# Both expert layers' first products: exact float32 matmuls replaced by three float32r passes over split operands

## The chip, the cores and the metric

The kernel runs on one core of a Trainium2 chip. The metric is the device time of one execution in microseconds (us). TensorE (PE) multiplies, VectorE (DVE) and ScalarE (ACT) work on tiles in SBUF and PSUM, GpSimd (POOL) issues the indirect transfers and SyncE (SP) most of the others. Every engine runs its own instruction list in order and waits on semaphores.

## The reference

Sixteen images of 256x256 pass through a wavelet stage, one attention layer, a first expert layer, a cosine "circuit" layer with a small feed-forward net, and a second expert layer, with a layer normalisation after each. Only the two expert layers matter here. Their core is, cut down:

```
# first expert layer: 4096 tokens, 8 experts, the best 2 of each token, hidden width 512
h = relu(einsum('nc,ech->neh', xf, w1) + b1)
expert_out = einsum('neh,ehc->nec', h, w2) + b2
out = einsum('ne,nec->nc', weights, expert_out)
# second expert layer: 8 experts, the best 1 of each token, hidden width 1024
h = gelu(einsum('ecd,edf->ecf', eb, W1) + b1[:, None, :], approximate=False)
y = einsum('ecf,efd->ecd', h, W2) + b2[:, None, :]
```

All inputs and outputs are float32; a token has 256 numbers.

## The kernel before

The stages follow each other: `attention`, `experts` (the first expert layer), `middle`, `last_experts` (the second). Between stages every engine waits for the others (`quiet0`, `quiet1`, `quiet2`).

Both expert stages work on tiles of 128 rows that all belong to one expert: 71 tiles in `experts`, 39 in `last_experts`. Rows were scattered to DRAM grouped by expert; a tile's rows come back by an indirect gather on POOL. The number of the tile's expert is computed on the chip (`tile_maps`, DVE) and read into a register of each engine that needs it (`value_load`). The computation of these maps is in two builds: the first 8 tiles (`maps_ok`), then the rest (`all_maps`).

One tile goes through these steps, and the order on PE is written out by hand:

- `g1(j)`: the first product, the transposed rows `xT` (128x128 twice) as stationary operand and the expert's first weights, 512 columns at a time, as moving operand. In `experts` that is two float32 matmuls (L1291), in `last_experts` four (L2054), in two halves of 512 columns.
- `x2(j+1)`: two PE transposes of the next tile's rows (L1282, L2042), which ACT copies into `xT` (L1338, L2100).
- `g2(j-1)`: the second product of the tile before, in four (L1303) or eight (L2065) float32 matmuls of 256 columns.
- `th(j)`: transposes of this tile's hidden values (L1313, L2075), which ACT passes through Relu (L1344) or Gelu (L2108, one instruction of 512 columns for each half).

DVE adds the first bias when it copies the first product out of PSUM (`eh`, L1383 and L2138), finds in `owner` which rows are whose (L1371 to L1376, the last one scales the row by a gate), and adds the second bias and combines in `g2` (L1392, L1396; L2147 to L2161). In `last_experts` it also normalises (`end`, L2169), after POOL has computed the root.

SBUF is cut into zones that the stages reuse. The first experts' weights take 64 KB a partition, the last experts' all 128 KB. Weights of four of the last experts are loaded during `middle`, the others at the start of `last_experts`.

Of the kernel before, what the change touches and what calls it, by code (L numbers as in the profile page):

```python
# [97 lines left out]
def tower(nc, a, out):  # L98
# [14 lines left out]
    def zones(stage):  # L113
        wide = Space(nc, low, W_BYTES, stage)
        return {"w": wide, "low": Space(nc, low, W_BYTES // 2, stage), "high": Space(nc, high, W_BYTES // 2, stage),
                "bias": Space(nc, bias, BIAS_BYTES, stage), "rest": Space(nc, rest, fixed - rest, stage),
                "open": Space(nc, bias, fixed - bias, stage), "free": Space(nc, bias + BIAS_BYTES // 4, fixed - bias - BIAS_BYTES // 4, stage)}

    with ctx:
# [21 lines left out]
        weights0 = zone0["low"]("w0", [P, E, 2 * F0 + F0 // P * D])  # L141
        zone_m = zones("_m")
        sb = zone_m["high"]
# [7 lines left out]
        bias1 = zone1["bias"]("b1", [P, E, F1 + D])  # L151
# [16 lines left out]
        def load_bias(sp, layer, to, e, landed):  # L168
            width = (F0, F1)[layer]
            for at, n, w in ((0, "b1", width), (width, "b2", D)):  # L170
                sp.dma_start(to[:, e, at:at + w], a[f"L{layer}_ffn_{n}"][e:e + 1, :].broadcast_to([P, w])).then_inc(landed, 16)

        def load_fixed(sp):
            for to, n in ((w2n, "attn_w2"), (w1n, "attn_w1"), (wg1, "ffn_wg")):
                sp.dma_start(to[:], a["L1_" + n].rearrange("(c p) k -> p c k", p=P)).then_inc(s["w_in_m"], 16)
            sp.dma_start(b1n[:], a["L1_attn_b1"].rearrange("(c p) -> p c", p=P), allow_slow_non_contiguous=True).then_inc(s["w_in_m"], 16)
# [3 lines left out]
        with nc.Block() as block:  # L180
            used = attention(nc, block, a, s, zones("_a"), ctx0, load_weights, lambda sp, e: load_bias(sp, 0, bias0, e, s["b_in0"]), h0_d, rows0_d, ident, before, ones, iota8, cnt,
                             lane, tile_no, ones8, sends0, minus_half)
            experts(nc, block, s, ctx, used, zone0, weights0, bias0, load_fixed, rows0_d, y0_d, cnt, ident, iota8, lane, tile_no, ones8)
            ctx0.close()
            middle(nc, block, a, s, ctx, zone_m, fixed_weights, load_weights, lambda sp, e: load_bias(sp, 1, bias1, e, s["w_in1"][e]), y0_d, rows1_d, ident, before, ones, iota8, cnt, away1, rank1, minus_half)
            last_experts(nc, block, s, ctx, zone1, weights1, bias1, load_weights, load_bias, rows1_d, gate1_d, out, cnt, rank1, away1,
# [3 lines left out]
def tile_maps(nc, c, sb, count, cnt, iota8, lane, tile_no, ones8):  # L190
# [40 lines left out]
    def maps(first_done, all_done):  # L231
        common()
        build(0, EARLY)
        c.eng.sem_inc(first_done, 1)
        build(EARLY, count)
# [4 lines left out]
def attention(nc, block, a, s, zone, sems, load_weights, load_bias, h0_d, rows0_d, ident, before, ones, iota8, cnt, lane, tile_no, ones8, sends0,  # L240
# [17 lines left out]
    with ExitStack() as psum:  # L258
# [8 lines left out]
        h1 = [sb(f"h1_{u}", [P, TPI, ROW0]) for u in range(2)]  # L267
        row_i = [sb(f"row_i{u}", [P, TPI, 2], I32) for u in range(2)]
# [5 lines left out]
        res = sb("res", [P, TPI, D])  # L274
        sb = zone["open"]
# [914 lines left out]
def experts(nc, block, s, ctx, used, zone, w, b, load_fixed, rows_d, y_d, cnt, ident, iota8, lane, tile_no, ones8):  # L1190
# [9 lines left out]
    xT = [sb(f"exT{u}", [P, 2, P]) for u in range(2)]  # L1200
    h = [sb(f"eh{u}", [P, width]) for u in range(2)]
# [4 lines left out]
    result = sb("result", [P, D])  # L1206
    sent_to = [sb(f"sent_to{u}", [P, 1], I32) for u in range(YR)]
# [5 lines left out]
        sem("e" + n) for n in ("xT_ps", "xT_ok", "g_ps", "h_ok", "t_ps", "hT_ok", "y_ps", "y_ok", "own_ok", "biased"))  # L1213
    y_out = [sem(f"ey_out{u}") for u in range(YR)]
    x_in, w_in = s["x_in0"], s["w_in0"]

    with ExitStack() as psum:
# [14 lines left out]
        def _(pool):  # L1232
            c = Chain(pool, s["pool_c"])
            pool.wait_ge(s["quiet0"], 4)
            for u in range(XR):
                c.run(nc.gpsimd.memset(x[u][:], 0.0))
            pool.wait_ge(c.sem, c.n)
            for u in (s["rows_out0"], s["rows_out0_odd"]):
# [3 lines left out]
            def load(j):  # L1242
                if j == EARLY:
                    pool.wait_ge(all_maps, 1)
                if j >= XR:
                    pool.wait_ge(xT_ps, j - XR + 1)
                    pool.wait_ge(own_ok, j - XR + 1)
# [17 lines left out]
        def _(pe):  # L1265
# [11 lines left out]
            def x2(j):  # L1277
                pe.wait_ge(x_in[j % XR], 16 * (j // XR + 1))
                if j >= 2:
                    pe.wait_ge(xT_ok, j - 1)  # L1280
                for ch in range(2):
# [3 lines left out]
            def g1(j):  # L1285
                e = number[j]
                pe.wait_ge(xT_ok, j + 1)
                if j >= 2:
                    pe.wait_ge(h_ok, j - 1)
                for ch in range(2):  # L1290
                    last = nc.tensor.matmul(bank[1 + j % 2][:], xT[j % 2][:, ch, :],  # L1291
                                            w[:, bass.ds(e, 1), width * ch:width * (ch + 1)].rearrange("p a f -> p (a f)"),
                                            start=ch == 0, stop=ch == 1)
# [902 lines left out]
```

## Time and profile before

| | |
|---|---|
| Median of 3 runs | 1461.22 us (1459.81 to 1462.4) |
| Profiled execution | 1454.15 us |
| Its span | 1452.4 us |
| PE busy | 1262.1 us (87%) |
| DVE busy | 950.5 us (65%) |
| POOL busy | 717.7 us (49%) |
| ACT busy | 522.8 us (36%) |

The span is what the trace covers. `experts` issues its first matmul at 512.9 us and its last near 809 us, `last_experts` runs from about 1116 us to the end. A float32 matmul appears in the trace as two records, each with its own weight load. A record's duration includes the way through the array, so that durations of neighbours overlap; the distance between starts says what one costs.

### The profile page before, as it was taken

The page shows a single profiled execution, that of the slowest core. Times are in us where ns is not written, and L with a number is a line of the kernel's source. Part 1 is how long each engine was busy: PE and PEld are TensorE (multiplying, and loading weights), DVE is VectorE, ACT ScalarE, POOL GpSimd, SP SyncE. Part 2 cuts the span into 40 slices and gives each one's busy share as a digit, 9 for nine tenths or more (in the row PEclk, how much of TensorE's full clock was granted, in tenths as well). Part 3 has the DMA queues.
Part 4 walks back from the last instruction along what each step waited for, and adds up shares of the span by engine and source line. Part 5 has one row for each costly group of instructions (what it writes and reads, how often), then busy time and mean ns, then how long its engine had stood idle before and what let it go on. Part 6 is the DMA issues. An engine that isn't in the chain of part 4 may idle for free. (4 is left out here: it accounts for less than half of the span.)

```text
span 1452.4 us, 23662 instructions
## 1 busy us (share of the span) xinstructions
PE 1262.1 (87%) x6856; PEld 895.0 (62%) x6856; DVE 950.5 (65%) x2759; ACT 522.8 (36%) x999; POOL 717.7 (49%) x912
## 2 busy tenths in 40 slices
PE   1389889889999589999999479999894999999997
PEld 0256556566665356666676357777773676767665
DVE  6678888887876455555555579999975344444443
ACT  1136455445555112222222366665651211111111
POOL 6673384472322344454454345666664354454543
PEclk9879899889998689999999777778876999999999
DMA  6566666567874414112121433321000910110000
GB/s 177 90 105 106 111 105 102 85 105 130 162 126 135 150 54 114 61 63 66 62 65 42 132 103 122 92 70 44 15 16 34 336 61 29 33 33 28 27 17 13
DMA packets 88619, 124.23 MB, mean 86 GB/s; under 512 B 17824, under 2 KB 71726, under 8 KB 87728
## 3 DMA queue, kind: packets, MB, share of 16 engines
q1 hardware_dynamic: 68704, 83.04, 26.9%
q0 software_dynamic: 16416, 38.46, 8.2%
q10 hardware_dynamic: 3376, 1.22, 0.4%
q8 instruction: 62, 1.02, 0.3%
q14 instruction: 61, 0.50, 0.1%
HBM read 69.14 MB, written 29.44 MB: 68 GB/s over the span
## 5 line engine op out<-in xcount | busy, mean ns | idle before, releaser
L1093 DVE TENSOR_REDUCE top_a_a<-s_bank 128x4 f32<-128x1024 f32 x128 | 156.4, 1222 | 51.2 <-PE s_bank L738 50.0
L2054 PE MATMUL ebank<-w,exT 128*128 x312 | 143.4, 603 | 0.7 <-ACT exT L2100 0.7
L1611 PE MATMUL mbank<-w2T_m,fhT_m 128*128 128x256 f32 x512 | 142.3, 441 | 0.0
L2065 PE MATMUL ebank<-w,ehT 128*128 x624 | 141.2, 379 | 0.9 <-ACT ehT L2108 0.9
L917 ACT ACTIVATE prob_a<-s_bank 128x1024 f32<-128x1024 f32 x128 | 130.7, 1021 | 19.5 <-PE s_bank L759 18.9
L1291 PE MATMUL ebank<-w,exT 128*128 x284 | 135.5, 600 | 0.6 <-ACT exT L1338 0.6
L1303 PE MATMUL ebank<-w,ehT 128*128 x568 | 134.4, 380 | 0.8 <-ACT ehT L1344 0.8
L1248 POOL DMA_INDIRECT ex<-rows_d,tile_row x71 | 72.4, 1020 | 123.6 <-DVE ey L1376 110.6
L1611 PEld LDWEIGHTS mbank<-w2T_m,fhT_m 128*128 128x128 f32 x512 | 118.3, 231 | 22.9
L2065 PEld LDWEIGHTS ebank<-w,ehT 128*128 128x128 f32 x624 | 115.6, 190 | 15.7 <-issue 1.6
L649 POOL DMA_INDIRECT rows_d<-h_a,row_i_a x64 | 64.2, 1003 | 98.6 <-DVE row_i_a L1178 86.7
L1383 DVE TENSOR_TENSOR eh<-ebank,b 128x512 f32<-128x512 f32 x71 | 49.1, 691 | 96.2 <-PE ebank L1291 96.2
L1303 PEld LDWEIGHTS ebank<-w,ehT 128*128 128x128 f32 x568 | 102.5, 190 | 12.5 <-issue 1.5
L2138 DVE TENSOR_TENSOR eh<-ebank,b 128x512 f32<-128x512 f32 x78 | 53.9, 691 | 77.4 <-PE ebank L2054 77.4
L2054 PEld LDWEIGHTS ebank<-w,exT 128*128 128x128 f32 x312 | 57.3, 194 | 58.7 <-issue 58.7
L2108 ACT ACTIVATE ehT<-ebank 128x512 f32<-128x512 f32 x78 | 42.3, 594 | 138.6 <-PE ebank L2075 138.6
L1253 POOL DMA_INDIRECT y_d<-ey,sent_to x71 | 72.8, 1025 | 34.8 <-issue 20.4
L738 PE MATMUL s_bank<-ks_a,qs_a 48*128 48x256 f32 x512 | 67.4, 343 | 25.9 <-DVE top_a_a L1093 14.7
L1344 ACT ACTIVATE ehT<-ebank 128x512 f32<-128x512 f32 x71 | 42.4, 597 | 131.0 <-PE ebank L1313 131.0
L2147 DVE TENSOR_TENSOR ey<-ebank,b 128x256 f32<-128x256 f32 x39 | 16.6, 425 | 95.1 <-PE ebank L2065 95.1
L1522 POOL TENSOR_SCALAR rstd_m_m<-moments_m_m 128x2 f32<-128x2 f32 x64 | 25.9, 404 | 105.8 <-DVE minus_m_m L1789 75.8
L771 PE MATMUL av_bank<-prob_a,vx_a 128*32 128x256 f32 x1024 | 77.8, 427 | 0.4 <-ACT heads_a L924 0.4
(348 smaller groups left out, 2662.8 us busy)
## 6 DMA issues: line engine op xcount, KB each, us to landing
w<-in_L_ffn_W SPq DMA_DIRECT2D x16, 1024.0 KB, 10.4
qs_a<-parts_q_a SPq DMA_DIRECT2D x96, 128.0 KB, 4.5
ks_a<-parts_k_a SPq DMA_DIRECT2D x96, 128.0 KB
w<-in_L_ffn_w SPq DMA_DIRECT2D x16, 512.0 KB, 5.6
image_a<-in_x SPq DMA_DIRECT2D x4, 1024.0 KB, 7.8
ya_m<-y_d SPq DMA_DIRECT2D x16, 256.0 KB, 2.8
yb_m<-y_d SPq DMA_DIRECT2D x16, 256.0 KB, 3.1
b<-in_L_ffn_b SPq DMA_DIRECT2D x8, 512.0 KB, 8.9
```

Of the source, the lines that this page charges most:

```text
L649: pool.indirect_dma_start(out=rows0_d, out_offset=bass.IndirectOffsetOnAxis(ap=row_i[i % 2][:, t, k:k + 1], axis=0), in_=h1[i % 2][:, t, : ...
L738: last = nc.tensor.matmul(s1_bank[:, g, t * SEQ:(t + 1) * SEQ], qs[i % RING][rows, j, t * P:(t + 1) * P], ks[i % RING][rows, j, :], start= ...
L771: last = nc.tensor.matmul(av_bank[32 * j:32 * j + 32, 0:SEQ], vx[i % RING][:, t, head(k, j), :], prob[:, (2 * k + j % 2) % 4, j // 2, t, : ...
L917: nc.scalar.activation(prob[:, j % 4].rearrange("p g t s -> p (g t s)"), s2_bank[:].rearrange("p g s -> p (g s)"), ACT.Exp, scale=HD ** -0 ...
L1093: nc.vector.tensor_reduce(top[:, j].rearrange("p g t -> p (g t)"), s1_bank[:].rearrange("p g (t s) -> p (g t) s", t=TPI), axis=AX, op=ALU. ...
L1248: pool.indirect_dma_start(out=x[j % XR][:].bitcast(I32), out_offset=None, in_=rows_d, bounds_check=E * SLOTS - 1, oob_is_err=False, in_off ...
L1253: pool.indirect_dma_start(out=y_d, out_offset=bass.IndirectOffsetOnAxis(ap=sent_to[j % YR][:], axis=0), in_=y[j % YR][:], in_offset=None, ...
L1291: last = nc.tensor.matmul(bank[1 + j % 2][:], xT[j % 2][:, ch, :], w[:, bass.ds(e, 1), width * ch:width * (ch + 1)].rearrange("p a f -> p ...
L1303: last = nc.tensor.matmul(bank[4 + j % 2][:, 0:D], hT[j % 2][:, f, :], w[:, bass.ds(e, 1), at:at + D].rearrange("p a d -> p (a d)"), start ...
L1611: last = nc.tensor.matmul(b[:, t * D:(t + 1) * D], hT[:, f, t * P:(t + 1) * P], w2T[:, f, :], start=False, stop=f == FC - 1)
L2054: last = nc.tensor.matmul(bank[1 + n % 2][:], xT[j % 2][:, ch, :], w[:, bass.ds(e, 1), at:at + 512].rearrange("p a f -> p (a f)"), start=c ...
L2065: last = nc.tensor.matmul(bank[4 + j % 2][:, 0:D], hT[j % 2][:, f, :], w[:, bass.ds(e, 1), at:at + D].rearrange("p a d -> p (a d)"), start ...
```

## The change

A float32r matmul takes one pass over its columns, at a lower precision of the operands. The change writes each operand of the first product as a near part (the value rounded to float32r) plus a rest (value minus near part), and adds three products: near by near, near by rest, rest by near. The code:

- In `experts`, ACT rounds all first weights into `w0_near` in 16 pieces of 512 columns, two a tile after `th(j)`, and DVE writes the rests into `w0_low`, two a tile behind `g2(j-1)`. Tiles 0 to 8 (`WHOLE` = 9) still use the float32 matmuls. From tile 9 on `g1` is six float32r matmuls in place of two float32 ones; ACT's copy goes to a float32r tile and DVE makes its rest (`xl`). The gate's scaling moves from DVE (L1376) to ACT (`scaled`), and a gather's buffer is now freed by it.
- In `last_experts` the two parts are made for each tile anew, one tile ahead: ACT reads the next tile's expert number, copies the expert's column of first biases (`own_bias`), and rounds 4 pieces of 512 columns (`rounded`); DVE makes the 4 rests (`rest`), interleaved with the copies out of PSUM. `g1` is twelve float32r matmuls in place of four float32 ones and waits for the rests. The first bias moves from DVE's copy to the Gelu, which becomes 8 instructions of 128 columns with a bias operand instead of 2 of 512.
- At the start of `last_experts` the first tile's rests come between the two builds of the maps.
- The first biases of the last experts are loaded as columns (8 small transfers in `load_fixed`), no longer broadcast to all partitions. SBUF zones are laid out anew; `middle` computes the same.

```diff
@@ experts, PE
             def g1(j):
                 e = number[j]
-                pe.wait_ge(xT_ok, j + 1)
+                if j < WHOLE:
+                    pe.wait_ge(xT_ok, j + 1)
+                if j >= WHOLE:
+                    pe.wait_ge(xl_ok, j + 1 - WHOLE)
+                if j == WHOLE:
+                    pe.wait_ge(low_ok, len(PIECES))
...
+                    if j < WHOLE:
+                        last = nc.tensor.matmul(to, xT[j % 2][:, ch, :], own[0], start=ch == 0, stop=ch == 1)
+                    else:
+                        nc.tensor.matmul(to, xTn[j % 2][:, ch, :], own[0], start=ch == 0, stop=False)
+                        nc.tensor.matmul(to, xTn[j % 2][:, ch, :], own[1], start=False, stop=False)
+                        last = nc.tensor.matmul(to, xTl[j % 2][:, ch, :], own[0], start=False, stop=ch == 1)
...
@@ experts, ACT
+            def scaled(j):
+                u = j % YR
+                act.wait_ge(own_ok, j + 1)
+                nc.scalar.activation(y[u][:], x[j % XR][:, 0:D], ACT.Identity, bias=nought[:, 0:1], scale=own[u][:, 2:3]).then_inc(scaled_ok, 1)
+            def near(n):
+                e, at = PIECES[n]
+                if at == 0:
+                    act.wait_ge(w_in[e], 32)
+                nc.scalar.activation(wn[:, e, at:at + PIECE], w[:, e, at:at + PIECE], ACT.Copy).then_inc(near_ok, 1)
...
@@ experts, DVE
             for j in range(count + 1):
                 if j < count:
                     g1(j)
+                if WHOLE <= j + 1 < count:
+                    xl(j + 1)
+                if j < count:
                     owner(j)
                 if j >= 1:
                     g2(j - 1)
+                    for n in range(2 * j - 2, min(2 * j, len(PIECES))):
+                        low(n)
...
@@ last_experts, PE
             def g1(j):
                 e = number[j]
                 pe.wait_ge(q["w_ready"], e + 1)
-                pe.wait_ge(q["xT_ok"], j + 1)
+                pe.wait_ge(q["xl_ok"], j + 1)
+                pe.wait_ge(q["low_ok"], PER * (j + 1))
...
@@ last_experts, ACT
             def th(j):
...
-                    nc.scalar.activation(hT[j % 2][:, at:at + 4].rearrange("p c s -> p (c s)"), bank[6 + n % 2][:], ACT.Gelu)\
-                        .then_inc(q["hT_ok"], 1)
+                    for f in range(4):
+                        last = nc.scalar.activation(hT[j % 2][:, at + f], bank[6 + n % 2][:, f * P:(f + 1) * P], ACT.Gelu, bias=b1[j % 2][:, at + f:at + f + 1])
+                    last.then_inc(q["hT_ok"], 1)
...
             for j in range(count):
                 if j + 1 < count:
+                    own_bias(j + 1)
+                    for k in range(PER - 1):
+                        rounded(j + 1, k)
                     x2(j + 1)
+                    rounded(j + 1, PER - 1)
+                act.wait_ge(q["b1_ok"], j + 1)
                 th(j)
...
@@ last_experts, DVE
-            maps(q["maps_ok"], q["all_maps"])
+            maps(q["maps_ok"], q["all_maps"], first_rest)
...
+            xl(0)
             for j in range(count + 2):
                 if j < count:
-                    g1(j)
+                    for n in range(FB):
+                        if j + 1 < count:
+                            rest(j + 1, n)
+                        g1(FB * j + n)
+                if j + 1 < count:
+                    xl(j + 1)
+                    for k in range(FB, PER):
+                        rest(j + 1, k)
                 if j >= 2:
                     end(j - 2)
```

## Rows read from the trace of the kernel before

**Rows 1.** The page, chain that ended last: shares of the span by line.

```profile
PE ebank L2054 9%; PE ebank L2065 9%; PE ebank L2075 2%; PE ebank L2042 1%; DMA ex<-rows_d,tile_row 0%; DVE row_f L225 0%; PE mbank L1629 0%; POOL out_tower L2008 0%; PE mbank L1621 0%; DVE r_m L1869 0%; DVE z_m L1860 0%; DVE stats_m_m L1779 0%; POOL rstd_m_m L1526 0%; POOL rstd_m_m L1524 0%; DVE eh L2138 0%
```

**Rows 2.** Busy time by window: PE, PEld, DVE, ACT, POOL, then PE clock, DMA.

```profile
530.00:600.00 70.00, 70.00 (x309) 48.54 (x308) 39.60 (x120) 16.75 (x35) 34.99 (x35) 1.00 0.33 90
563.00:564.00 1.00, 1.00 (x6) 0.86 (x5) 0.87 (x5) 0.00 (x0) 0.03 (x1) 1.00 1.26 175
1250.00:1350.00 100.00, 100.00 (x432) 70.37 (x431) 42.88 (x99) 18.03 (x37) 49.46 (x63) 1.00 0.11 32
```

**Rows 3.** The chain in order of time, one tile of `last_experts`: start, us, what.

```profile
1143.02 3.43 PE ebank L2054 x8
1146.45 0.22 PE ebank L2042 x2
1146.67 3.46 PE ebank L2065 x16
1150.13 0.87 PE ebank L2075 x8
```

**Rows 4.** Timeline of one tile of `experts`: start, us, engine, line, what.

```profile
605.38 0.42 DVE L1392 TENSOR_TENSOR result<-ebank,b 128x256 f32<-128x256 f32 x1 [0.41 <-PE ebank L1303]
605.51 1.88 PE L1291 MATMUL ebank<-w,exT 128*128 x4
605.84 0.48 DVE L1396 SCALAR_TENSOR_TENSOR ey<-result,own,ey 128x256 f32<-128x256 f32 x1
607.23 0.38 PE L1282 MATMUL ebank<-ident,ex 128*128 128x128 f32 x2
607.61 0.69 DVE L1383 TENSOR_TENSOR eh<-ebank,b 128x512 f32<-128x512 f32 x1 [1.28 <-PE ebank L1291]
608.21 0.22 DVE L1371 SCALAR_TENSOR_TENSOR chosen<-ex,tile_sum 128x6 f32<-128x6 f32 x1
```

**Rows 5.** Timeline of `middle`: four float32r matmuls of 256 columns, 80 rows.

```profile
987.18 0.72 PE L1595 MATMUL mbank<-qT_m,wq_m 80*128 80x256 f32 x4
```

**Rows 6.** Groups by line and shape: count, busy us, mean ns, idle before.

```profile
L2100 ACT ACTIVATE exT<-ebank 128x256 f32<-128x256 f32 x39 | 15.0, 384 | 124.7 <-PE ebank L2042 124.7
L895 ACT ACTIVATE parts_k_a<-bank,bk_a 128x256 fp32r<-128x256 f32 x32 | 13.4, 471 | 31.6 <-PE bank L715 31.6
L1702 ACT ACTIVATE arg_size_m<-arg_m 128x512 f32<-128x512 f32 x16 | 10.1, 631 | 5.1 <-DVE arg_m L1809 5.1
L1818 DVE TENSOR_TENSOR sum_m<-prods_m,h_m 128x512 f32<-128x512 f32 x16 | 11.1, 692 | 0.5
```

**Rows 7.** Timeline: transposes and Gelu of one late tile; two ScalarE instructions behind each other.

```profile
1325.60 1.04 PE L2075 MATMUL ebank<-ident,eh 128*128 128x128 f32 x8
1326.30 1.09 ACT L2108 ACTIVATE ehT<-ebank 128x512 f32<-128x512 f32 x2 [3.57 <-PE ebank L2075]
332.67 0.84 ACT L895 ACTIVATE parts_k_a<-bank,bk_a 128x256 fp32r<-128x256 f32 x2 [1.29 <-PE bank L715]
```

**Rows 8.** PE's reading of a tile's expert number (L1275): ns min/median/max.

```profile
L1275 PEldq TENSOR_LOAD <-tile_expert x71: 297/369/510, 506.0 to 797.5; - x71
L1275 PEldq FUSED_REGOPS  x71: 151/151/165, 506.6 to 797.9; - x71
```

**Rows 9.** Timeline, start of `last_experts`: second map build, last DVE step, first product.

```profile
1121.87 0.42 DVE L218 TENSOR_TENSOR past<-tile_no,upto 128x248 f32<-128x248 f32 x1
1125.60 0.42 DVE L2124 TENSOR_REDUCE den<-exps 128x32 f32<-128x256 f32 x1
1126.55 0.18 DVE L2128 TENSOR_SCALAR outside<-outside 128x39 f32<-128x39 f32 x1
1126.84 6.65 PE L2054 MATMUL ebank<-w,exT 128*128 x8 [0.67 <-ACT exT L2100]
```

**Rows 10.** Two DVE lines, all instances: ns min/median/max.

```profile
L1396 DVE SCALAR_TENSOR_TENSOR ey<-result,own,ey x71: 483/485/494, 523.8 to 809.9; 128x256 f32<-128x256 f32 x71
L225 DVE TENSOR_SCALAR row_f<-row_f,lane x4: 231/246/2022, 504.8 to 1124.2; 128x8 f32<-128x8 f32 x2, 128x63 f32<-128x63 f32 x1, 128x31 f32<-128x31 f32 x1
```

More of the change, by code:

```diff
@@ L116, in zones @@
                 "bias": Space(nc, bias, BIAS_BYTES, stage), "rest": Space(nc, rest, fixed - rest, stage),
-                "open": Space(nc, bias, fixed - bias, stage), "free": Space(nc, bias + BIAS_BYTES // 4, fixed - bias - BIAS_BYTES // 4, stage)}
+                "open": Space(nc, bias, fixed - bias, stage),
+                "after": Space(nc, bias + 4 * E * (F0 + D) + 32 * (F1 // P), fixed - bias - 4 * E * (F0 + D) - 32 * (F1 // P), stage),
+                "above": Space(nc, bias + 4 * E * (F0 + D), BIAS_BYTES - 4 * E * (F0 + D), stage)}
     with ctx:
@@ L234, in maps @@
         c.eng.sem_inc(first_done, 1)
+        if between:
+            between()
         build(EARLY, count)
@@ L1350, in _ @@
                 th(j)
+                scaled(j)
+                for n in range(2 * j, min(2 * j + 2, len(PIECES))):
+                    near(n)
             nc.scalar.drain().then_inc(s["quiet1"], 1)
@@ L1919, in last_experts @@
     out_v = out.rearrange("i s d -> (i s) d")
-    sb = zone["rest"]
+    PIECE, PER = 512, 2 * width // 512
+    near = [zone["bias"](f"near{u}", [P, 2 * width], F32R) for u in range(2)]
+    sb = zone["after"]
+    low = [sb(f"low{u}", [P, 2 * width], F32R) for u in range(2)]
+    b1 = [sb(f"b1_own{u}", [P, FC]) for u in range(2)]
     x = [sb(f"ex{u}", [P, WIDE_ROW]) for u in range(XR)]
-    xT = [sb(f"exT{u}", [P, 2, P]) for u in range(2)]
+    xT, xTl = ([sb(f"{n}{u}", [P, 2, P], F32R) for u in range(2)] for n in ("exT", "exTl"))
     h = [sb(f"eh{u}", [P, 512]) for u in range(HR)]
@@ L2053, in g1 @@
                         at = width * ch + 512 * (n % FB)
-                        last = nc.tensor.matmul(bank[1 + n % 2][:], xT[j % 2][:, ch, :],
-                                                w[:, bass.ds(e, 1), at:at + 512].rearrange("p a f -> p (a f)"), start=ch == 0, stop=ch == 1)
+                        to, whole, rest = bank[1 + n % 2][:], near[j % 2][:, at:at + 512], low[j % 2][:, at:at + 512]
+                        nc.tensor.matmul(to, xT[j % 2][:, ch, :], whole, start=ch == 0, stop=False)
+                        nc.tensor.matmul(to, xT[j % 2][:, ch, :], rest, start=False, stop=False)
+                        last = nc.tensor.matmul(to, xTl[j % 2][:, ch, :], whole, start=False, stop=ch == 1)
                     last.then_inc(q["g_ps"], 1)
@@ new lines, in first_rest @@
+            def first_rest():
+                dve.wait_ge(q["exps_ok"], 1)
+                c.link(nc.vector.tensor_reduce(den[:], ex[:], axis=AX, op=ALU.add))
+                c.link(nc.vector.reciprocal(den[:], den[:]))
+                nc.vector.scalar_tensor_tensor(out=gates[:], in0=rank[:], scalar=float(CAP), in1=den[:], op0=ALU.is_lt, op1=ALU.mult)\
+                    .then_inc(q["gates_ok"], 1)
+                for k in range(PER):
+                    rest(0, k)
+            maps(q["maps_ok"], q["all_maps"], first_rest)
```

142 lines of the change are left out of this document (92 added, 50 removed).

## The prediction

> **What bounds the kernel now.** I read the chain of waits first: it is PE almost alone, and PE's four lines of `last_experts` hold 21% of the span, the stage's whole length [rows 1]. The busy time by window then says where PE has no gap: 70.00 of 70 us in `experts` and 100.00 of 100 in `last_experts`, both at a granted clock of 1.00, its 2.4 GHz level [rows 2]. In these stretches time is the sum of what PE has in its list, and no other engine is waited for. ACT is busy 24% and 18% there, DVE 57% and 43%. The chain in order of time gives a late tile: first product 3.43, `x2` 0.22, second product 3.46, `th` 0.87, together 7.98 us for each of 39 tiles [rows 3]. In `experts` the first product takes 607.23 - 605.51 = 1.72 us [rows 4]; with `x2` 0.22, half the late tile's second product (1.73) and half its `th` (0.44), all from [rows 3], a tile takes 4.1 us, 71 times. So what shortens the first product shortens the kernel, as long as nothing else becomes late.
>
> **Price of a float32r pass.** A float32 matmul of 512 columns is two records, 3.43/8 = 0.43 us apart, so 0.86 us each [rows 3]. Float32r matmuls are in the trace with 256 columns and 80 rows: four take 0.72 us, and less about 0.28 for the last one's way through the array that is 0.44/3 = 0.15 between starts on average, a first handover among them [rows 5]. The second product's records also go through 512 columns (two times 256) in 3.46/16 = 0.216 us. I take 0.215 us for a pass of 512. Twice the 0.15 would be 0.29, and the far end is 0.43, the spacing of one float32 record, if operands of 128 rows cannot be streamed faster. I take the row with as many columns, since columns are what the float32 records' spacing follows (256 twice 0.216, 512 twice 0.43).
>
> **`experts`.** From tile 9 on `g1` is six passes, 6 x 0.215 = 1.29, in place of 1.72 us: 0.43 less for each of 62 tiles, **-26.7 us**. The other engines have room. DVE gets `xl` (0.43, as the 256 columns of L1392) and loses L1376; ACT gets `scaled` and, until tile 7, two pieces of 0.63 us a tile (as L1702 [rows 6]), against a tile of 4.1 us of which it uses a quarter. `x2` is ready 1.3 us into a tile, ACT's copy takes 0.38 [rows 6], DVE's `eh` and `xl` end by about 2.8 of 3.67, so `g1(j+1)` finds its rest.
>
> One wait is not hidden. Tile 9's `g1` wants all 16 rests, and the last two are behind `g2(7)` on DVE in the turn of tile 8. In the turn shown, the same step (L1396) starts 0.33 us after PE's `g1` and ends at 606.32 [rows 4]; in the tile numbering of the change that `g1` is tile 9's. Two rests of 0.69 us (L1818 [rows 6]), 0.61 apart as L1383 and its successor are [rows 4], end at 606.32 + 0.61 + 0.69 = 607.62, against a start at 605.51: **+2.2 us**, once. It is 0 if the queue turns out shorter.
>
> **`last_experts`, PE.** Twelve passes are 2.58 in place of 3.43 us: a tile of 7.12 us if nothing waits, 0.86 less.
>
> **`last_experts`, the loop through ACT and DVE.** Here two lightly used engines get most of PE's relief as work. ACT: 8 Gelus of 128 columns with a bias. 256 columns without one take 0.384, with one 0.471, and the second of two starts 0.84 - 0.47 = 0.37 behind the first [rows 6, 7]; L2108's pair gives 0.49 for 512 columns [rows 7]. That is 0.83 ns a column, so a Gelu of 128 costs 0.37 - 0.11 = 0.26 to 0.27 between starts and 0.37 in full. Rounding takes 0.63 in full (L1702 [rows 6]) and about 0.53 between starts. Reading the expert number is 0.37 + 0.15 and small change on PE [rows 8]; I take 0.6. ACT's sum is 8 x 0.27 + 4 x 0.53 + 0.3 + 0.6 + 0.15 = 5.3 us of 7.1. DVE has 42.88/100 x 7.98 = 3.4 us a tile now [rows 2] and gets 4 x 0.69 + 0.43 = 3.2: 6.6 busy, less where neighbours overlap. Neither sum exceeds PE's, but both lists are in order, and this path closes over two tiles:
>
> - `th(j-1)` starts at 0. ACT's first Gelu starts 0.70 later (1326.30 against 1325.60 [rows 7]), the eighth 7 x 0.27 later, at 2.6.
> - Behind it the expert number, 0.6, and the bias copy: 3.4. The first near part of tile j+1 is ready at about 4.1.
> - DVE waits for it in front of both `eh` copies of tile j. With 0.2 for the wait and the address (L1383 starts 0.22 after PE's end at 607.39 [rows 4]), rest 0, `eh`, rest 1, `eh`, `xl`, rest 2, rest 3 start at 4.3 + 0, 0.61, 1.22, 1.83, 2.44, 2.78, 3.39, and the last ends at 8.38.
> - `g1(j+1)` can start at 8.44, and `th(j+1)`, the same step two tiles on, 7.12 - 0.87 = 6.25 later.
>
> Two tiles then take 8.44 + 6.25 = 14.69, one 7.35 us, more than PE's 7.12. So I expect DVE's rests to be waited for about 0.2 us a tile and a gain of 7.98 - 7.35 = 0.63 over 38 periods: **-23.9 us**. Bounds: no wait at all, -32.7. With no overlap of Gelus (0.37 each) the path is 0.7 longer; with 0.2 more per rest (L1396's 0.485 for 256 columns, doubled, is the nearest row with overheads counted twice) 0.8 more. Both give (14.69 + 1.5)/2 = 8.1 and +4.6.
>
> One rule of the Trainium skill speaks against DVE's new work: GPSIMD Engine Reference, section Specifications, says that POOL's SBUF interfaces are shared with VectorE and contend with its instructions that have two SBUF inputs, which every rest is. The trace shows such a hold-up: L225, 0.23 us elsewhere, took 2.02 while POOL filled buffers, though it has one tensor input; it also shows L1396, with two SBUF inputs and next to POOL's gathers, at 483 to 494 ns in all 71 instances [rows 10]. By the rows the rests keep 0.69 us; by the rule each could be held by a gather's issue.
>
> **Start of `last_experts`.** Before, DVE makes the second map build under the first gather's flight, 1121.87 to 1125.60, and ends at 1126.73; `g1(0)` starts at 1126.84 [rows 9]. Now the first rests come between the builds. ACT reads the number and rounds four pieces from 1121.8: 0.6 + 0.15 + 3 x 0.53 + 0.63, so 1124.8; the last rest starts at 1125.1, the second build at 1125.7, and takes 3.7; `outside` and `xl(0)` 0.6, so `g1(0)` starts at about 1130.1: **+3.3 us**. The tail after the last tile's products is unchanged.
>
> **At nothing.** Eight bias columns are 8 x 1024 elements of 4 bytes on SP's queue, which has no other work then; PE was busy 1.00 of 1 us at a DMA share of 1.26 while the like was loaded [rows 2]. If gathers are held longer than the buffers last, a few us. The gather's buffer is freed about 2 us later by `scaled`; four buffers of 3.67 us cover this. The gate's scaling on ACT, bias adds, new zones and the larger count in `middle`'s waits are off PE's path. A dynamic address now stands before six matmuls; PE reads ahead of its array, cover that would cost tenths of a us a tile if gone.
>
> **Sum.** -26.7 + 2.2 - 23.9 + 3.3 = -45.1 us. The profiled execution would be 1454.15 - 45.1 = 1409. It is 7.1 us below the median of the runs; the same difference on that median gives 1461.22 - 45.1 = **1416 us**.
>
> **The rivals.**
> - *No wait on the rests.* If reading the number overlaps the last Gelus, the path is up to 0.5 shorter and PE alone bounds: -26.7 + 2.2 - 32.7 + 3.3 = -54, 1407. For it: both sums are below 7.1. Against: the rests stand before and behind both copies in order. 0.15.
> - *ACT and DVE bound the last experts*, 7.6 to 8.1 us a tile: between -36 and -17, 1426 to 1445. For it: three new handovers whose latency I priced from two rows. 0.2.
> - *Slower, by POOL.* POOL issues three indirect transfers a tile at 1.0 us. If the rests wait for them, DVE's 6.6 us become 9.6 and set the tile: -24.5 + 38 x 1.6 + 3.3 = +40, 1501. The gain is gone from 8.5 us a tile on. L1396 speaks against, L225 for it [rows 10]. It is what the rule named above, of the Trainium skill's GPSIMD Engine Reference, would do here. 0.05.
> - *Slower, by the pass.* If a float32r pass of 128 rows costs 0.43, the first products grow by 62 x 0.86 + 39 x 1.73 = 121 us, 1582. The change would then not do what it says. Against: the spacing with 80 rows [rows 5]. 0.04.
> - *No change, by the pass.* At 0.29 us a pass the first products take 3.48 and 1.74 us, as now; with the two delays that is 1461 + 8 at most, within 0.5%, and about the same if one of them is smaller. 0.02.
> - My forecast, 7.2 to 7.6 us a tile, 1410 to 1426: 0.54.
>
> **The range.** 1403 to 1438: down to no wait with a free start, up to most of the second rival; 0.13 lies outside, the two slower rivals among it. A run of this kernel tells about 0.2%, 3 us, from no change. Faster by more: 0.89; within it 0.02 (a pass of nearly 0.29 us); slower 0.09.
>
> **What would show each step.** Passes in `g1` 0.215 us apart in both stages; `g1` to `g1` 4.1 us until tile 8 and 3.67 after; one gap near 2 us before tile 9; in `last_experts` PE idle about 0.2 us a tile before `g1`, released by DVE's rest, alternating or even; the ACT list full to about 75%, rests at 0.69 us with and without POOL beside them; the first product of `last_experts` some 3 us later after the maps. I am wrong if rests are longer beside POOL, if PE waits for ACT's Gelu instead, or if the passes are further apart.

## The result and the profile after

The changed kernel takes 1424.68 us (median of 4 runs, 1422.47 to 1425.59), the kernel before in the same session 1460.51 (4 runs, 1459.12 to 1462.4): a ratio of 0.9752, 95% interval 0.9735 to 0.9769, so 35.8 us less. The forecast was 45.1 us less.

The profiled execution of the change is 1425.59 us long, only 28.6 less than the one of before. That difference can't be used as it stands. I cut both traces at the same matmuls (between the first two stages lie 12 us more, alike in all four). "The maps" is the first DVE step of `tile_maps` in `last_experts`:

| stage, us | before | change | second profile of each |
|---|---|---|---|
| start to last matmul of attention | 500.8 | 507.4 | 505.1, 502.7 |
| `experts`, first to last PE start | 296.1 | 279.6 | 296.1, 278.2 |
| from there to the maps of `last_experts` | 307.6 | 307.2 | 305.9, 305.2 |
| maps to the end | 335.8 | 317.8 | 335.1, 317.7 |

Over all thirteen profiles of this study the attention, whose instructions are the same in all kernels here (from the change on, some of its tiles lie elsewhere in SBUF), ends anywhere between 500.2 and 510.7 us, and the third stage takes 304 to 308. The second and fourth repeat within 1.5 us for one and the same code. So the change's worth is read from these two. The first profiles give -16.5 and -18.0 us, -34.5 together; the second ones -17.9 and -17.4, -35.3. Two things that aren't the change's stand in these sums: two odd tiles (below) in the change's first profile, 1.4 us, and the clock in the second profile of before. `last_experts` starts with TensorE partly at its 1.2 GHz level (granted clock 0.55 from 1126.84 to 1133.50 in the first profile of before, 0.53 from 1119.70 to 1126.00 in the change), but 0.68 from 1129.41 to 1136.00 in the second profile of before, whose first tile took 7.18 us where the others had 8.03, 8.15 and 8.20. With -17.9, which has no odd tiles, and -18.0, which has the like clock in both, it is -35.9; the medians say -35.8.

The page, then its chain of waits by line, answers to [rows 1]: PE's four lines of the stage are now six, with 21% as before, and DVE's rest (`low`) is on the chain, with a share that rounds to nothing.

```profile
span 1423.9 us, 25417 instructions
...
PE 1220.6 (86%) x7136; PEld 949.3 (67%) x7136; DVE 1059.0 (74%) x2961; ACT 692.2 (49%) x1515; POOL 733.0 (51%) x913
...
PE ebank L2130 9%; PE ebank L2118 3%; PE ebank L2120 3%; PE ebank L2119 3%; PE ebank L2140 2%; PE ebank L2104 1%; DVE low L2221 0%; DVE row_f L230 0%; ACT ehT L2174 0%; PE mbank L1690 0%; POOL out_tower L2070 0%; PE mbank L1682 0%; DVE r_m L1930 0%; DVE z_m L1921 0%; DVE stats_m_m L1840 0%
```

Busy time by window, beside [rows 2]: PE is still full, DVE went from 43 to 80 us in 100 and ACT from 18 to 64. POOL's 49 have become 58, of which more below.

```profile
620.00:690.00 70.00, 70.00 (x373) 59.61 (x372) 44.52 (x132) 26.89 (x55) 38.74 (x38) 1.00 0.21 68
1200.00:1300.00 100.00, 99.98 (x517) 85.55 (x516) 79.65 (x179) 63.70 (x190) 58.06 (x67) 1.00 0.11 34
```

The chain in order of time through one late tile, beside [rows 3]. Twelve passes stand where eight float32 records took 3.43 us. They are 0.23 apart, and the first one after the transposes takes longer (0.31 and 0.29 here): this is where the rest is waited for. In parts_once, below, where nothing is waited for, it has 0.23 to 0.24.

```profile
1275.28 0.87 PE ebank L2140 x8
1276.15 0.31 PE ebank L2118
1276.46 0.23 PE ebank L2119
1276.69 0.23 PE ebank L2120
...
1278.97 0.22 PE ebank L2104 x2
1279.19 3.46 PE ebank L2130 x16
1282.64 0.87 PE ebank L2140 x8
1283.52 0.29 PE ebank L2118
```

The timeline of ACT and DVE in that tile (groups of equal instructions are one line with their count):

```profile
1278.18 0.21 ACT L2187 ACTIVATE b_own<-b_cols_m 128x8 f32 x1 [0.17 <-issue]
...
1278.30 1.66 ACT L2191 ACTIVATE near<-w 128x512 fp32r x3
...
1279.06 0.69 DVE L2221 TENSOR_TENSOR low<-w,near 128x512 fp32r<-128x512 f32 x1 [1.24 <-ACT near L2191]
...
1279.67 0.68 DVE L2244 COPY eh<-ebank 128x512 f32<-128x512 f32 x1
...
1281.80 1.28 DVE L2221 TENSOR_TENSOR low<-w,near 128x512 fp32r<-128x512 f32 x2
...
1282.48 1.04 PE L2140 MATMUL ebank<-ident,eh 128*128 128x128 f32 x8
...
1283.20 2.17 ACT L2174 ACTIVATE ehT<-ebank,b_own 128x128 f32<-128x128 f32 x8 [2.46 <-PE ebank L2140]
...
1283.34 0.47 PE L2118 MATMUL ebank<-near,exT 128*128 128x512 f32 x1
...
1285.54 0.21 ACT L2187 ACTIVATE b_own<-b_cols_m 128x8 f32 x1 [0.17 <-issue]
...
1285.65 0.62 ACT L2191 ACTIVATE near<-w 128x512 fp32r x1
```

The last rest ends at 1283.08 and the first pass starts 0.26 us later. A tile of this stage takes 7.38 us (7.983 before), a tile of `experts` 3.779 (4.103).

Tile 9 of `experts` in the timeline shows the one long wait, 2.06 us on PE, and behind which work the last two rests stood:

```profile
558.14 0.60 PE L1340 MATMUL ebank<-ident,eh 128*128 128x128 f32 x4
...
558.45 0.42 DVE L1447 TENSOR_TENSOR result<-ebank,b 128x256 f32<-128x256 f32 x1 [0.29 <-PE ebank L1330]
...
558.91 0.48 DVE L1451 SCALAR_TENSOR_TENSOR ey<-result,own,ey 128x256 f32<-128x256 f32 x1
...
559.32 1.29 DVE L1433 TENSOR_TENSOR w_low<-w,w_near 128x512 fp32r<-128x512 f32 x2
...
560.81 0.49 PE L1318 MATMUL ebank<-w_near,exTn 128*128 x1 [2.06 <-issue]
...
561.13 0.39 PE L1319 MATMUL ebank<-w_low,exTn 128*128 x1
...
561.37 0.39 PE L1320 MATMUL ebank<-w_near,exTl 128*128 x1
...
561.60 0.39 PE L1318 MATMUL ebank<-w_near,exTn 128*128 x1
...
561.83 0.39 PE L1319 MATMUL ebank<-w_low,exTn 128*128 x1
```

The second of the two rests ends at 559.32 + 1.29 = 560.61 and the product starts 0.20 later. From the second pass on the passes are 0.23 to 0.24 apart.

### The profile page after: what moved, and what is told of

Read it like the earlier page. It is cut to its first block and busy times, and to the rows that moved or that the text cites. A ratio compares the mean times of both kernels' runs of the same rounds, so it can differ in the third digit from the quotient of the medians.

```text
span 1423.9 us, 25417 instructions
## 1 busy us (share of the span) xinstructions
PE 1220.6 (86%) x7136; PEld 949.3 (67%) x7136; DVE 1059.0 (74%) x2961; ACT 692.2 (49%) x1515; POOL 733.0 (51%) x913
## 3 DMA queue, kind: packets, MB, share of 16 engines
q1 hardware_dynamic: 75872, 78.87, 26.7%
## 5 line engine op out<-in xcount | busy, mean ns | idle before, releaser
L2221 DVE TENSOR_TENSOR low<-w,near 128x512 fp32r<-128x512 f32 x156 | 103.7, 686 | 49.6 <-ACT near L2191 49.3
L2174 ACT ACTIVATE ehT<-ebank,b_own 128x128 f32<-128x128 f32 x312 | 84.7, 383 | 96.0 <-PE ebank L2140 84.1
L1372 ACT ACTIVATE ehT<-ebank 128x512 f32<-128x512 f32 x71 | 42.6, 600 | 130.3 <-PE ebank L1340 114.8
L1427 DVE TENSOR_TENSOR eh<-ebank,b 128x512 f32<-128x512 f32 x71 | 49.1, 692 | 68.8 <-PE ebank L1320 58.6
L2191 ACT ACTIVATE near<-w 128x512 fp32r x156 | 88.8, 617 | 0.2 <-issue 0.2
L745 PEld LDWEIGHTS s_bank<-ks_a,qs_a 48*128 48x128 f32 x512 | 41.7, 200 | 55.8 <-issue 30.2
L2118 PE MATMUL ebank<-near,exT 128*128 128x512 f32 x156 | 65.1, 418 | 5.8 <-DVE exTl L2237 4.4
L649 POOL TENSOR_SCALAR rstd_a_a<-moments_a_a 128x2 f32<-128x2 f32 x16 | 5.4, 340 | 119.5 <-DVE moments_a_a L1136 119.5
```

Of the source, the lines that this page charges most:

```text
L745: last = nc.tensor.matmul(s1_bank[:, g, t * SEQ:(t + 1) * SEQ], qs[i % RING][rows, j, t * P:(t + 1) * P], ks[i % RING][rows, j, :], start= ...
L2118: nc.tensor.matmul(to, xT[j % 2][:, ch, :], whole, start=ch == 0, stop=False)
L2174: last = nc.scalar.activation(hT[j % 2][:, at + f], bank[6 + n % 2][:, f * P:(f + 1) * P], ACT.Gelu, bias=b1[j % 2][:, at + f:at + f + 1])
L2191: nc.scalar.activation(near[j % 2][:, at:at + PIECE], w[:, bass.ds(number[j], 1), at:at + PIECE].rearrange("p a f -> p (a f)"), ACT.Copy)\
L2221: nc.vector.tensor_tensor(low[j % 2][:, at:at + PIECE], w[:, bass.ds(number[j], 1), at:at + PIECE].rearrange("p a f -> p (a f)"), near[j % ...
```

## The experiments

The kernel before had medians between 1456.6 and 1460.7 us in the sessions of these runs, so two kernels are compared by their ratios to it and by their stages. All stages are from the profile of each.

**before_again, after_again.** Both kernels unchanged, one profile more of each.

> The kernel before, unchanged, once more with a profile. Its first expert tile is gathered by 512.9 us in the first profile, 6.4 us earlier than in the changed kernel's (519.3), and that execution (1454.15 us) is 6.4 us faster than the median of its timed runs (1460.51). If attention's length varies from execution to execution, this profile's span may have attention end anywhere from 501 to 507 us with the same code, and the stages behind it unchanged: 296.1 us from the first transposes of the first experts to their last, 334.7 us from the maps of the last experts to the end. If instead the change itself lengthened attention (its tiles lie elsewhere in SBUF), this profile repeats the 500.8 us of the first.

> The changed kernel, unchanged, once more with a profile. If attention's length is chance, its last matmul starts somewhere between 501 and 507 us, not necessarily at 507.4 as in the first profile; if the change lengthened it, at 507.4 again. The two late tiles of the first experts that took 4.02 and 4.96 us in place of 3.78 (+1.4 us together) recur at the same tile if something in the program causes them, and not if it was chance. The stall before tile 9 (2.0 us) and the 7.38 us a tile of the last experts recur in either case.

1455.87 and 1417.47 us, one run each. Their stages are in the table above: attention's length goes with the execution and not with the change (505.1 without it, 502.7 with it), and only the two touched stages differ by a fixed amount. The two odd tiles of the first profile (59 and 60 of `experts`, 4.02 and 4.96 us) are not in the second.

**experts_exact.** The products of `experts` stay float32 for all 71 tiles; the last experts are as in the change.

```diff
-    WHOLE = 9
+    WHOLE = 71
...
-                if j == WHOLE:
-                    pe.wait_ge(low_ok, len(PIECES))
```

> The first experts' products stay exact float32 for all 71 tiles, the rest of the change stays: the parts of the weights are still made in the first nine tiles, and nobody uses them. Parts of the gain by the two profiles: the first experts' stage 16.5 us, the last experts' 18.0. So this kernel should lose 62 x (4.10 - 3.78) - 2.0 - 1.4 = 16.5 us against the changed one and come to about 1441 us, ratio 0.987 to the kernel before; its last experts as in the change, 7.38 us a tile. By the prediction's own prices (0.215 us a pass) the loss would be 24.5 us, 1449 us. If what ACT and DVE do more in the first experts (scaling, rounding) cost PE anything, the tiles would be above 4.10 us.

1438.08 us median (1436.09 to 1443.65), ratio 0.9886 (0.9852 to 0.9919). `experts` takes 296.1 us and 4.103 a tile, as before, though ACT and DVE still make the parts of the weights and ACT scales (the rest of each tile's rows, `xl`, isn't made, since no tile uses it); the last stage takes 318.0, as in the change. The two halves of the gain are independent.

**halves.** In `experts` each three-pass product of 512 columns is cut into two of 256, so twelve passes in place of six for the same columns.

```diff
-                for ch in range(2):
...
+                for half in range(2 if j >= WHOLE else 0):
+                    for ch in range(2):
...
+                        cut = slice(256 * half, 256 * half + 256)
+                        nc.tensor.matmul(to[:, cut], xTn[j % 2][:, ch, :], own[0][:, cut], start=ch == 0, stop=False)
```

> In the first experts each float32r pass of 512 columns is cut into two of 256, twelve for a tile in place of six, same arithmetic. A pass of 512 took 0.2305 us between starts, 0.017 more than 512 columns at 2.4 a ns, where the second product's float32 records stay at 0.2155. Theory A: every float32r instruction has a fixed extra of about 0.015 us (its weight load cannot be overlapped whole). Then six more instructions cost 62 x 6 x 0.015 = +5.6 us. Theory B: the extra is per column, at about 0.45 ns a column, as the 0.1175 us of the 256-column float32r matmuls in the middle stage suggest. Then two halves cost 0.235, and the kernel grows by 62 x 6 x 0.0045 = +1.7 us.

1420.09 us (1418.59 to 1422.96), ratio 0.9753 (0.9724 to 0.9783). A tile takes 3.817 us, 0.038 more for six more instructions, 0.006 us each: +2.4 us over 62 tiles, nearer to theory B (+1.7) than to A (+5.6). The passes of 256 columns start 0.119 apart:

```profile
644.35 0.28 PE L1319 MATMUL ebank<-w_near,exTl 128*128 x1
644.47 0.28 PE L1317 MATMUL ebank<-w_near,exTn 128*128 x1
644.59 0.28 PE L1318 MATMUL ebank<-w_low,exTn 128*128 x1
644.71 0.28 PE L1319 MATMUL ebank<-w_near,exTl 128*128 x1
```

So of the 0.016 us by which a pass of 512 exceeds my price, about 0.006 goes with the instruction and 0.010 with its columns.

**parts_once.** In the last experts ACT and DVE make parts for the first two tiles only; later tiles multiply with what the buffers hold. This leaves out the parts of each tile from the third on, and PE's wait for their rests; DVE still reads each tile's expert number.

```diff
-                    for k in range(PER - 1):
+                    for k in range(PER - 1 if j == 0 else 0):
...
-                        if j + 1 < count:
+                        if j == 0:
                             rest(j + 1, n)
```

> In the last experts the near parts and rests are made for tiles 0 and 1 only, and every later tile multiplies with those two sets: the output is that of wrong weights from tile 2 on, and 37 tiles' rounding on ACT and subtraction on DVE (2.5 and 2.7 us a tile) are left out. PE's list is the same. Theory PE: the twelve passes at 0.23 us alone set the 7.38 us a tile, then nothing changes. Theory loop (the prediction's): the two-tile path through ACT and DVE sets it, g1 starting 0.25 us after the last rest every time; then PE alone gives th 0.79 + g1 2.83 + x2 0.22 + g2 3.45 = 7.29 us, 0.09 less, and the kernel is 38 x 0.09 = 3.4 us faster.

1415.93 us (1413.88 to 1418.29), ratio 0.9714 (0.9697 to 0.973). A tile takes 7.308 us: PE alone. In the chain from one first pass to the next:

```profile
1268.08 0.23 PE ebank L2118
...
1275.39 0.24 PE ebank L2118
```

DVE is busy 49.47 and ACT 38.42 us in 100, and the passes are 0.23 apart as ever, so the rests and the roundings beside them are not what makes them 0.23. The change's 7.38 hold 0.07 us of waiting.

**round_twice.** ACT rounds the first piece of each tile twice, and waits for the end of the first rounding, on the path to the first rest.

```diff
+            def again(j):
...
+                act.wait_ge(q["again_ok"], j)
...
                     own_bias(j + 1)
+                    again(j + 1)
```

> In the last experts ACT rounds the first piece of each tile twice, one behind the other: about 0.75 us more between the end of the Gelus and the first rest. Theory loop: the path th(j-1) to g1(j+1) closes over two tiles and is just critical, so a tile grows by half of it, 0.37 us, 38 tiles +14 us. Theory PE: ACT has over a us to spare a tile, nothing changes or up to the slack only. Theory single: if the path closed over one tile, +0.75 each, +28 us.

1430.72 us (1427.61 to 1432.46), ratio 0.9819 (0.9799 to 0.9839). A tile takes 7.71 us in the mean, most of them 7.64 to 7.72, and from tile 14 on nine alternate between 7.94 to 7.99 and 7.41 to 7.43. From one tile's transposes to the product two tiles on it takes 8.88 us in place of 8.22. So a tile has 0.33 more for 0.66 more on the path: the path closes over two tiles.

**number_early.** ACT reads a tile's expert number one tile ahead, in front of the Gelus.

```diff
-                number[j] = e = act.value_load(tile_expert[0:1, j:j + 1], min_val=0, max_val=E - 1)
+                e = number[j]
...
+                if j + 2 < count:
+                    read_number(j + 2)
                 act.wait_ge(q["b1_ok"], j + 1)
                 th(j)
```

> In the last experts ACT reads the next-but-one tile's expert number before the Gelus instead of behind them, where it waits for the transposes anyway. About 0.45 us leaves the path from the Gelus to the first rest (0.58 us between the last Gelu's start and the bias copy's, of which about 0.15 remains). Theory loop: the path falls below PE's own 7.29 us a tile, so the gain is 0.09 us a tile, 3.4 us in all, and PE's list is the bound. Theory PE: no change.

1419.7 us (1419.34 to 1420.11), ratio 0.9744 (0.9727 to 0.976). Nothing moves: 7.38 us a tile, and the bias copy still starts 0.58 us behind the last Gelu's start. The reading, which I had priced at 0.6, was hidden under the Gelus. What holds the copy is its wait for the Gelus that still read the bias buffer it would overwrite: it cannot start before the last one is complete (0.38 us) and has told of it.

**round_first.** number_early, and the rounding before the bias copy. The rounding needs neither the last Gelu nor the bias.

```diff
-                    own_bias(j + 1)
+                    may_round(j + 1)
                     for k in range(PER - 1):
                         rounded(j + 1, k)
                     x2(j + 1)
                     rounded(j + 1, PER - 1)
+                    own_bias(j + 1)
```

> The expert number of the last experts is read a tile ahead on ACT, and the near parts stand before the copy of the bias columns in ACT's list; the copy comes last in its turn. If the loop through ACT and DVE sets 7.38 us a tile because the first near part waits for the last Gelu's completion (0.38) and the bias copy (0.2 and a handover), the first near part starts about 0.25 instead of 0.70 us behind the last Gelu's start, the loop's 14.77 us over two tiles become 14.32, less than PE's two times 7.307, and a tile takes 7.31 us: 38 x 0.07 = -2.8 us in this stage, a ratio near that of the change less 0.002. Rival: if the wait comes from the rests' places behind eh on DVE and not from the first near part's time, the tile stays at 7.38 and nothing changes.

1421.14 us (1419.53 to 1426.37), ratio 0.974 (0.9717 to 0.9763). The timeline shows the eight Gelus from 1263.72 (the last starts at 1265.51), the rounding 0.22 us behind that where it was 0.68 in the change (1285.65 - 1284.97), and the copy out of the way:

```profile
1263.72 2.17 ACT L2174 ACTIVATE ehT<-ebank,b_own 128x128 f32<-128x128 f32 x8 [2.69 <-PE ebank L2140]
...
1265.73 1.72 ACT L2197 ACTIVATE near<-w 128x512 fp32r x3
...
1267.56 0.68 ACT L2197 ACTIVATE near<-w 128x512 fp32r x1
...
1268.08 0.26 ACT L2193 ACTIVATE b_own<-b_cols_m 128x8 f32 x1
...
1404.67 5.40 PE L2130 MATMUL ebank<-w,ehT 128*128 x16 [2.01 <-ACT ehT L2174]
```

A tile takes 7.308 us, PE's own floor, as expected. That is 2.6 us over 38 periods (278.6 in place of 281.2), and yet the stage has only 1.1 less (316.7). The rest of it was given back at the very end, by the clock and not by the edit: the last second product, the last row above, took 5.40 us where the change had 3.72. Busy time by window in it: PE stays busy, the granted clock falls to 0.75 and 0.64, a mixture of the 2.4 and the 1.2 GHz level.

```profile
1404.67:1407.00 2.33, 2.33 (x8) 2.01 (x9) 0.41 (x1) 0.00 (x0) 1.32 (x2) 0.75 0.05 15
1407.00:1410.10 3.10, 3.07 (x9) 2.13 (x8) 0.00 (x0) 0.00 (x0) 0.00 (x0) 0.64 0.00 0
```

**build_first.** DVE makes the second map build before the first rests and not between the builds.

```diff
         c.eng.sem_inc(first_done, 1)
-        if between:
-            between()
         build(EARLY, count)
         c.eng.sem_inc(all_done, 1)
+        if between:
+            between()
```

> DVE builds the second map of the last experts before the first tile's rests, as the kernel before did, and not between. Theory: the start costs 13.9 us from the maps to the first product because five steps on DVE stand one behind the other; put first, the build overlaps ACT's first four near parts (about 3 us) and the first gather, and the rests follow: first product after about 12.8 us, -1.1 us. Rival: the near parts are late anyway, the start is a sum over the same engine, and nothing changes (within 0.3 us).

1421.23 us (1421.06 to 1430.15), ratio 0.9757 (0.9729 to 0.9785). From the maps to the first product 13.76 us where the change has 13.94: nothing changes within 0.3 us, as the rival said, but not for its reason. In the change DVE sits idle for 0.75 us before its first rest, for ACT's first near part. With the build in front that part is ready in time, and yet 0.57 us pass before the first rest, in which the profile shows no wait for another engine. Otherwise DVE does the same steps in either order.

**whole10.** The parts of all weights are used from tile 10 on.

```diff
-    WHOLE = 9
+    WHOLE = 10
```

> The first experts switch to float32r passes at tile 10 instead of tile 9. The stall of 2.0 us in front of tile 9, for the last two rests, goes; one more tile costs 4.10 in place of 3.78 us. So 2.0 - 0.33 = 1.7 us less in the stage. If the stall moved with the switch (a wait for something other than the rests), +0.3 us.

1419.62 us (1417.39 to 1420.83), ratio 0.9746 (0.973 to 0.9763). The wait of 2 us is gone; `experts` takes 276.8 us with one odd tile 0.55 too long, so 276.2 against 278.2: the wait's 2.2 less the 0.24 that tile 9 no longer gains (4.02 us where it had 3.78).

**best.** whole10, build_first and round_first together.

```diff
...
-    WHOLE = 9
+    WHOLE = 10
...
+                    may_round(j + 1)
...
+                    own_bias(j + 1)
```

> Three edits together: the parts of all weights whole from tile 10 on in place of 9, the second map's build before the first rests, and the near parts before the bias copy with the number read ahead. If they add up: -1.9 (no stall, less one tile's gain: -2.0 + 0.3), -1.1 and -2.8, about -5.5 us against the change in the two stages, 276.5 + 313.5 us where the change has 278.2 + 317.7, and a median near 1415. If the loop's theory is wrong, 317 us in the last stage and about -3 in all.

1421.75 us (1418.96 to 1424.54), ratio 0.9733 (0.9714 to 0.9751). Tiles take 3.779 and 7.31, no wait at tile 9; the stages 277.6 and 316.9. The first has 1.4 us of odd tiles and the second 1.7 of the slower last product; without them they would be 276.2 and 315.2. The attention of this profile ended at 510.7, the latest of all. The median near 1415 that I expected was missed: the 1.1 us of build_first did not come, and in the profiled execution the odd tiles, the clock at the end and the late attention came on top. The 4.5 us that the edits are worth by the stages are smaller than what the untouched stages do from run to run, and the intervals of best and of the change overlap: that it beats the change is read from its tiles, not shown by the medians.

## Why the prediction was right, point by point

The direction and the mechanism were right, and the measured time lies in the range, in the part of it that I called my forecast (7.2 to 7.6 us a tile, 1410 to 1426). One of my signs of being wrong did come: the passes are further apart than 0.215. The forecast was 9 us too hopeful, and the terms say where ("38 periods" is from the first tile's first product to the last tile's, the tail what follows):

| term | forecast | measured |
|---|---|---|
| a float32r pass of 512 columns | 0.215 | 0.231 (`experts`), 0.230 (last experts) |
| `experts`, 62 tiles | -26.7 | 62 x (4.103 - 3.779) = -20.1 |
| wait before tile 9 | +2.2 | +2.2 (2.06 of PE idle) |
| 38 periods of last experts | -23.9 | 303.4 to 281.2 = -22.2 |
| start of last experts | +3.3 | 10.24 to 13.94 = +3.7 |
| tail | 0 | 22.17 to 22.69 = +0.5 |
| sum | -45.1 | -35.9 |

**The mis-sized term is the price of a float32r pass.** I took a float32 record of the second product (0.216), counting its 256 columns twice, for a pass of 512. A float32r pass is 0.016 us longer, 7%. Six of them make 1.39 us and not 1.29; over 62 tiles that is about 6 of the 6.6 us that this term is off. The same in the last experts is 12 x 0.015 = 0.18 a tile for PE alone (7.31 and not 7.12). The better row was there. The float32r matmuls that I had in [rows 5] averaged 0.15 between starts of 256 columns, a handover among them. Taken one by one in the same trace they start at 987.18, 987.39, 987.50 and 987.62: 0.117 to 0.118 apart after the handover, twice which is 0.235 for 512 columns, 0.004 from what was measured. halves shows 0.119, twice which is 0.238.

**The loop was right in its shape and right in size partly by luck.** From one tile's transposes to the product that waits for the rests I forecast 8.44 us; the trace has 1283.34 - (1282.48 - 7.36) = 8.22. From that product to the transposes two tiles on I forecast 6.25; the chain above has 1282.64 - 1276.15 = 6.49, and 6.51 is the median of the late tiles. The sum is 14.73, against 14.69 forecast and 2 x 7.38 = 14.76 measured. In the first part the reading of the number cost nothing where I had 0.6, and in its place stood a wait that I had not priced, for the last Gelu's completion; in the second part the passes were longer. That the loop closes over two tiles is shown by round_twice, and that the copy's wait was in it by round_first, whose tiles lost it. The rival without a wait was wrong by little: PE's own sum moved up to 7.31 and left 0.07 us of waiting in place of the 0.2 that I expected.

**The other engines' sums.** DVE is busy 0.7965 x 7.38 = 5.9 us a tile where I had 6.6, ACT 0.637 x 7.38 = 4.7 where I had 5.3. ACT's 0.6 is the reading of the number, which is no busy time; that neighbours on DVE overlap more than I granted is argued, not shown. The start of the stage has its steps as forecast, each about 0.4 us later: the last rest 8.9 us behind the maps (8.5 by the prediction), the second build 9.5 (9.1), the first product 13.9 (13.5).

**The tail** was not unchanged. Eight Gelus of 128 columns now follow the last transposes, where two of 512 did, and nothing covers them there. From the start of the last tile's transposes to that of its second product there are 3.04 us in place of 1.92, 1.1 more; the last tile's shorter first product pays back 0.6. The Gelus' price per tile, which I worked out from [rows 6, 7], was right (0.25 between starts, 0.38 in full, against 0.26 to 0.27 and 0.37); I had not asked where it lies bare.

**The rivals.** ACT and DVE as the bound (7.6 us or more) did not come; round_twice, at 7.71, shows what it takes: 0.65 us more on the path. The pass at 0.29 or 0.43 did not either. For the hold-up by POOL: all rests in the window from 1200 to 1300 us, of which POOL is busy for 58, are between 675 and 727 ns, and so are all 156 of the stage (in round_first, build_first and best a few reach 750 to 770):

```profile
L2221 DVE TENSOR_TENSOR low<-w,near x54: 675/683/727, 1200.3 to 1297.1; 128x512 fp32r<-128x512 f32 x54
```

POOL paid, not DVE. Two of its three transfers a tile, by line in a window of 260 us: the kernel before, then the change, then parts_once. (The third, `out_tower`, has 1125, 1187 and 1124 ns.)

```profile
L1985 POOL DMA_INDIRECT ex<-rows_d,tile_row x32 | 33.6, 1048 | 9.6 <-issue 9.6
L1994 POOL DMA_INDIRECT egate<-gate_d,ex x32 | 30.8, 962 | 9.8 <-issue 9.5 <-DVE eres L2169 0.3
```

```profile
L2047 POOL DMA_INDIRECT ex<-rows_d,tile_row x32 | 42.0, 1313 | 9.8 <-issue 9.8
L2056 POOL DMA_INDIRECT egate<-gate_d,ex x36 | 39.7, 1103 | 11.0 <-issue 11.0
```

```profile
L2056 POOL DMA_INDIRECT egate<-gate_d,ex x36 | 34.6, 962 | 12.3 <-issue 12.3
L2047 POOL DMA_INDIRECT ex<-rows_d,tile_row x32 | 33.4, 1045 | 9.8 <-issue 9.8
```

The gather of the rows takes 1313 ns beside the parts' work, and 1048 and 1045 where there is none. parts_once leaves out ACT's roundings with DVE's rests, so this row alone doesn't say which of them holds it. The gather of the gates does: it runs beside rests for 0.9 us on average and beside roundings for 0.01, and it grew from 962 to 1103 ns. This costs nothing here, since POOL is busy for only 58% of the time. The rule of the Trainium skill that I weighed (GPSIMD Engine Reference, section Specifications: the SBUF interfaces contend when a VectorE instruction has two SBUF inputs) agrees in so far as the two disturb each other; that VectorE's instruction would be the one that is held, the reading on which my rival stood, these rows contradict. Whether the way is by those interfaces no row shows.

Beside POOL's fills of buffers, at the start of the stage, two short DVE steps of one tensor input each are held again (the second perhaps only behind the first), as L225 was in [rows 10]. The same section of the Trainium skill's GPSIMD Engine Reference also names VectorE instructions in a 2-port perf mode as contending; whether L230 is one no trace here shows:

```profile
1108.48 2.01 DVE L230 TENSOR_SCALAR row_f<-row_f,lane 128x8 f32<-128x8 f32 x1
1108.62 1.87 DVE L231 TENSOR_REDUCE limit<-past_part 128x8 f32<-128x64 f32 x1
```

## What to carry to other kernels

When PE is the only bound, price its new instruction from records of the same kind, taken one by one without their handovers, and then ask what 10% of error does to the sum: here one price stood in 62 x 6 and 39 x 12 places and made most of the miss. When lightly used engines get work in front of a bound one, write the path down from semaphore to semaphore and see over how many tiles it closes; in each turn put what feeds the bound engine before what waits for the turn's own end, as the rounding before the bias copy. And compare two profiles stage by stage: here the whole executions said 28.6 us and the touched stages 35.9.

## What the runs showed of the hardware

- A float32r matmul of 512 columns and 128 rows starts 0.231 us after the one before, one of 256 columns 0.119. A float32 record is 0.216 for 256 columns and 0.43 for 512, as if it were two passes of 0.108 and 0.215. So a float32r pass is 7 to 10% dearer than half a float32 record. Neighbours don't make it so: the 15 passes of `experts` in three profiles (after, after_again, parts_once) beside which neither ACT nor DVE worked are 0.231 to 0.232 apart as well. Why is open.
- The last second product ran partly at the 1.2 GHz level in 5 of the 13 profiles and took 1.7 us more: seven or eight of its sixteen records are 0.43 apart in place of 0.22, after PE had been idle for 2.01 us. In the other profiles of changed kernels the same idle time stood in front of it (in the two of the kernel before one that is 1.1 shorter), and the clock stayed at 1.00. What decides between them no run shows.
- In four profiles (after, round_first, build_first, best) the tiles 59 and 60 of `experts` took 4.0 and 5.0 us, 1.4 more together, in the others not. ACT and DVE had both been idle and resumed within 0.01 us of each other, for a reason that the trace gives only as remote; ACT's copy of the rows 3 us earlier had already been late by about 1 us. The cause stays open.

```profile
751.88 0.42 DVE L1447 TENSOR_TENSOR result<-ebank,b 128x256 f32<-128x256 f32 x1 [1.65 <-remote]
751.89 0.60 ACT L1372 ACTIVATE ehT<-ebank 128x512 f32<-128x512 f32 x1 [2.63 <-remote]
```

- The attention, with the same instructions in all thirteen profiles, ended between 500.2 and 510.7 us after the start; two executions of one kernel differ by over 4 us (500.8 and 505.1, 507.4 and 502.7). This is more than the gain of any edit tried here after the change itself, and it stays open.
